# A mixture-of-experts transformer kernel: the routing steps inside attention spread over other engines, and the PSUM banks of scores and maxima exchanged

## The reference

```python
x = x + attention(layernorm(x), Wq, Wkv_down, Wk_up, Wv_up, Wo)       # 8 heads of 32, softmax over 1024 keys
x = x + moe_top2(layernorm(x), gate_w, w1, b1, w2, b2)                # 14 experts, the two best of a softmax
x = x + linear_attention(layernorm(x), Wq, Wk, Wv, Wo)                # 16 heads of 8, cumulative sums
x = x + moe_top1(layernorm(x), router_w, W1, b1, W2, b2)              # 8 experts, capacity 1280
```

```python
probs = softmax(x @ gate_w.T)
top2_p, top2_i = top_k(probs, 2)
w = top2_p / maximum(top2_p.sum(-1, keepdims=True), 1e-10)
moe_out = w[:, 0:1] * out_of(top2_i[:, 0]) + w[:, 1:2] * out_of(top2_i[:, 1])
```

## Time and profile before

| | us |
|---|---|
| median of 3 runs | 2246.83 (2245.2 to 2247.13) |
| profiled execution | 2234.0 |
| its span | 2232.3 |
| mean granted clock of TensorE in it, share of full | 0.887 |
| busy in the span: PE / DVE / ACT / POOL | 1722.2 / 1527.5 / 1177.9 / 1366.9 |

### The profile page before, as it was taken

How to read it: one execution, slowest core, us unless ns; L and a number is a source line. 1 busy time by engine, 2 the same in 40 slices (tenths; PEclk the granted TensorE clock), 3 DMA queues, 4 the chain that set the end, 5 groups by cost and what they waited for, 6 DMA issues and landing times. The chain is left out here.

```text
span 2232.3 us, 54806 instructions
## 1 busy us (share of the span) xinstructions
PE 1722.2 (77%) x18737; PEld 1007.6 (45%) x18737; DVE 1527.5 (68%) x3787; ACT 1177.9 (53%) x2275; POOL 1366.9 (61%) x1088
## 2 busy tenths in 40 slices
PE   7977999998989899898952799377767776100997
PEld 3423455444444444444432688344444443000897
DVE  5756888899889889888835234178888877620453
ACT  4625887877777677777741355224444444021343
POOL 0004777766778777777785233488888872155465
PEclk9977999999999999999975799688999988555999
DMA  4754222221313122222222434400000000132332
GB/s 154 247 170 139 60 69 79 59 81 55 93 57 95 58 72 79 60 90 62 78 78 76 156 125 122 152 21 20 19 19 19 19 19 0 43 114 77 99 102 63
DMA packets 161611, 178.39 MB, mean 80 GB/s; under 512 B 39905, under 2 KB 124776, under 8 KB 161416
## 3 DMA queue, kind: packets, MB, share of 16 engines
q1 hardware_dynamic: 146584, 145.41, 21.3%
q0 software_dynamic: 13824, 29.43, 4.0%
q10 hardware_dynamic: 1008, 0.92, 0.1%
HBM read 97.76 MB, written 78.16 MB: 79 GB/s over the span
## 5 line engine op out<-in xcount | busy, mean ns | idle before, releaser
L941 DVE TENSOR_REDUCE halfmax<-p_m 128x1 f32<-128x512 f32 x1024 | 657.5, 685 | 122.3 <-PE p_m L694 111.0
L922 ACT ACTIVATE probs<-p_s,ESCALE 128x512 f32<-128x512 f32 x1024 | 645.9, 689 | 103.8 <-PE p_s L718 84.5
L632 POOL TENSOR_TENSOR sum_p<-sum_p,probs 128x1024 f32<-128x1024 f32 x192 | 455.7, 2374 | 38.9 <-ACT probs L922 25.4
L694 PE MATMUL p_m<-ka,qa 96*32 96x512 f16 x4096 | 422.6, 396 | 40.2 <-DVE halfmax L941 26.3
L718 PE MATMUL p_s<-qa,ka 98*32 98x512 f16 x4096 | 417.5, 388 | 15.9 <-DMA qa<-max_lo 10.7
L725 PE MATMUL p_o<-probs,vh 128*32 128x256 f32 x4096 | 320.0, 384 | 0.4 <-ACT probs L922 0.4
L632 POOL TENSOR_TENSOR sum_p<-probs 128x1024 f32<-128x1024 f32 x64 | 151.6, 2369 | 217.9 <-ACT probs L922 217.5
L694 PEld LDWEIGHTS p_m<-ka,qa 96*32 96x32 f16 x4096 | 114.3, 95 | 302.8 <-DVE halfmax L941 247.5
L1653 PE MATMUL ln_p_cum<-ln_kv,c_tri 128*128 128x512 f32 (+1 forms) x384 | 169.8, 587 | 89.6 <-POOL ln_kv L1597 89.6
L1306 ACT ACTIVATE e_h<-e_p_h,e_w 128x256 f32<-128x256 f32 x316 | 126.8, 474 | 159.3 <-PE e_p_h L1285 85.3
L718 PEld LDWEIGHTS p_s<-qa,ka 98*32 98x32 f16 x4096 | 118.2, 97 | 112.0 <-ACT probs L922 25.3
(11 more groups left out here) (298 smaller groups left out, 2740.6 us busy)
## 6 DMA issues: line engine op xcount, KB each, us to landing
e_xb<-xs SPq DMA_DIRECT2D x40, 257.0 KB
e_xb<-xs SPq DMA_DIRECT2D x78, 128.0 KB, 2.0
ys<-e_y SPq DMA_DIRECT2D x78, 128.0 KB, 1.9
v<-pj_v SPq DMA_DIRECT2D x8, 1024.0 KB, 5.0
qa<-q SPq DMA_DIRECT2D x64, 128.0 KB
ka<-k SPq DMA_DIRECT2D x64, 128.0 KB
vh<-v SPq DMA_DIRECT2D x64, 128.0 KB
o<-ot SPq DMA_DIRECT2D x64, 128.0 KB
```

The lines of the kernel that those rows point to most:

```text
L632: nc.gpsimd.tensor_tensor(sum_p[i][:, :], (sum_p[i] if n else probs[0])[:, :], probs[k][:, :], ALU.add).then_inc(sum_p_d, 1)
L694: mm = nc.tensor.matmul(max_bank(s, n)[j * DH0:(j + 1) * DH0, :], qa[s][0:KA, (n // 2) * P + j * DH0:(n // 2) * P + (j + 1) * DH0], ka[s][ ...
L922: nc.scalar.activation(probs[k][:, h * HALF:(h + 1) * HALF], score_bank(u % SLOTS, k, h)[:, :], ACT.Exp, scale=ESCALE[:, 0:1]).then_inc(pr ...
L941: nc.vector.reduce_max(halfmax[u % 2][:, n // 2, n % 2:n % 2 + 1], max_bank(u % SLOTS, n)[:, :], AX.X).then_inc(max_read, 1)
```

## The change

The kernel after differs in these points.

- **Banks**: `p_s` has two banks and `p_m` three. `SCORE_BANKS` alternates over two, `MAX_BANKS` rotates over three.
- **`best_two`**: the sums go to `totals`, one column per tile of the whole run; `prob` stays unscaled, and the reciprocal and the scaling fall away there.
- **`find_experts`** keeps the eight `max_index` alone. Two ScalarE copies (`keep_bests`, `keep_chosen`, piece 9) store the two best values in `GATE` and the two indices in `chosen`. **`mark_chosen`** (VectorE, piece 9) writes `hot` by 16 `tensor_scalar` of 14 elements, each comparing `steps`, an iota stored with step 2, with one column of `chosen`. **`join_marks`** (GpSimd, piece 10, behind its fourth sum and its scatter) adds both halves of `hot` into `both`.
- **`count_tiles`** is gone. **`ranks`** moves from piece 11 to 10 and carries the counts in PSUM: one matmul of the identity with `base` (the row numbers reached so far), one of `stri` with `both`, and eight of `ones` with one tile of `both` broadcast over the tiles behind it, 112, 98, ..., 14 columns. The ninth block of `pos_ps` is the new `base`, which ScalarE copies in `keep_base` (piece 12).
- **`find_slots`** moves from piece 12 to 11 and is a product of `hot` with `pos_ps` and one reduction into `tabs["slotf"]`. GpSimd converts these to the integers of `slot`. The scatters start at piece 13 instead of 14.
- **`gates`** runs once, on all tiles, behind `find_rows`. The last matmul for the counts is replaced by `base - start`.
- For the last two batches `mark_experts` does the marks and `both` on VectorE in three instructions.

```diff
-SCORE_BANKS = tuple(i % 3 for i in range(SLOTS * SCORES - 4)) + (0, 1, 0, 2)
-MAX_BANKS = tuple(i % 2 for i in range(SLOTS * RING))
+SCORE_BANKS = tuple(i % 2 for i in range(SLOTS * SCORES))
+MAX_BANKS = tuple(i % 3 for i in range(SLOTS * RING))
...
             def scatter(h, half):
...
+                if n == 0:
+                    pool.wait_ge(places, 2 * b + 2)
+                    nc.gpsimd.tensor_copy(slot[b % NX][:, :], tabs["slotf"][:, b * ST * 2:(b + 1) * ST * 2]).then_inc(slot_d, 1)
                 apart(pool, slot_d, b + 1, passed)
...
+            def join_marks(b):
+                pool.wait_ge(marks_d, b + 1)
+                from_first(pool, pos_d, b)
+                nc.gpsimd.tensor_tensor(both[:, :, :], hot[:, 0, :, :], hot[:, 1, :, :], ALU.add).then_inc(hot_d, 1)
...
                 pe.wait_ge(hot_d, b + 1)
-                pe.wait_ge(seen_d, (b + 1) * ST)
-                nc.tensor.matmul(pos_ps, c["stri"][:, :], both[:, :, :], start=True, stop=False)
-                nc.tensor.matmul(pos_ps, c["ones"][:, :], seen[:, 0:ST, :], start=False, stop=True).then_inc(pos_d, 1)
+                from_first(pe, base_d, b)
+                nc.tensor.matmul(pos_ps, c["ident"][:, :], base[:, :].unsqueeze(1).broadcast_to([P, ST + 1, E0]),
+                                 start=True, stop=False, skip_group_check=True)
+                nc.tensor.matmul(pos_ps[:, 0:ST, :], c["stri"][:, :], both[:, :, :], start=False, stop=False, skip_group_check=True)
+                for t in range(ST):
+                    mm = nc.tensor.matmul(pos_ps[:, t + 1:ST + 1, :], c["ones"][:, :], both[:, t:t + 1, :].broadcast_to([P, ST - t, E0]),
+                                          start=False, stop=(t == ST - 1), skip_group_check=True)
+                mm.then_inc(pos_d, 1)
...
+            def keep_bests(b):
+                act.wait_ge(choice, 2 * b + 2)
+                nc.scalar.copy(GATE[:, b * ST * 2:(b + 1) * ST * 2].rearrange("p (t k) -> p t k", k=2), best[:, :, 0:2]).then_inc(gates_d, 1)
+
+            def keep_chosen(b):
+                act.wait_ge(best_d, b + 1)
+                from_first(act, marks_d, b)
+                nc.scalar.copy(chosen[:, :, :].rearrange("p k t -> p t k"), at[:, :, 0:2]).then_inc(chosen_d, 1)
+
+            def keep_base(b):
+                act.wait_ge(pos_read, b + 1)
+                nc.scalar.copy(base[:, :], pos_ps[:, ST, :]).then_inc(base_d, 1)
...
+            def mark_chosen(b):
+                if b == 0:
+                    dve.wait_ge(set_d, 3)
+                dve.wait_ge(chosen_d, b + 1)
+                from_first(dve, pos_read, b)
+                for k in range(2):
+                    for t in range(ST):
+                        last = nc.vector.tensor_scalar(hot[:, k, t, :], steps[:, :, 0], chosen[:, k, t:t + 1], None, ALU.is_equal)
+                last.then_inc(marks_d, 1)
...
             def find_slots(b):
                 dve.wait_ge(pos_d, b + 1)
-                nc.vector.tensor_tensor(place[:, :, :], pos_ps, start[:, :].unsqueeze(1).broadcast_to([P, ST, E0]), ALU.add).then_inc(pos_read, 1)
+                nc.vector.tensor_tensor(placed[:, :, :, :], hot[:, :, :, :],
+                                        pos_ps[:, 0:ST, :].unsqueeze(1).broadcast_to([P, 2, ST, E0]), ALU.mult).then_inc(pos_read, 1)
                 dve.wait_ge(pos_read, b + 1)
...
+                nc.vector.tensor_reduce(tabs["slotf"][:, b * ST * 2:(b + 1) * ST * 2].rearrange("p (t k) -> p k t", k=2), placed[:, :, :, :],
+                                        AX.X, ALU.add).then_inc(places, 2)
```

More of the change, by code:

```diff
@@ L457, in attend @@
         xT = sb("r_xT", [P, GT])
-        top, total, prob = sb("r_top", [P, G]), sb("r_total", [P, ST]), sb("r_prob", [P, ST, E0])
+        top, totals, sums, prob = sb("r_top", [P, G]), sb("r_totals", [P, TILES]), sb("r_sums", [P, TILES]), sb("r_prob", [P, ST, E0])
+        chosen, steps = sb("r_chosen", [P, 2, ST]), sb("r_steps", [P, E0, 2])
         best, at = sb("r_best", [P, ST, 8]), sb("r_at", [P, ST, 8], U32)
[L460 to L464, removed]
+        hot, both = sb("r_hot", [P, 2, ST, E0]), sb("r_both", [P, ST, E0])
+        now, start, base = sb("r_now", [P, E0]), sb("r_start", [P, E0]), sb("r_base", [P, E0])
+        placed = sb("r_placed", [P, 2, ST, E0])
         zeros = sb("r_zeros", [P, BT // P, D])
@@ L637, in head @@
                         scatter(u, n - 2)
+                    marked = sequence(u, 10)
+                    if n == 3 and marked is not None and marked < B - 2:
+                        join_marks(marked)
             for s in range(SLOTS):
@@ L649, in _ @@
                 normalise(u)
-            for h in range(UNITS, FIRST + 14 + B * H0):
+            for h in range(UNITS, FIRST + 13 + B * H0):
                 for half in range(2):
@@ L904, in behind_tile @@
                         exponentials(b)
+                    b = sequence(h, 9)
+                    if b is not None:
+                        keep_bests(b)
+                        if b < B - 2:
+                            keep_chosen(b)
+                    b = sequence(h, 12)
+                    if b is not None:
+                        keep_base(b)
             act.sem_inc(od_d, OD0)
@@ new lines, in mark_experts @@
+            def mark_experts(b):
+                dve.wait_ge(best_d, b + 1 + (b - B + 2))
+                from_first(dve, pos_read, b)
+                for k in range(2):
+                    last = nc.vector.scalar_tensor_tensor(out=hot[:, k, :, :], in0=at[:, :, k].unsqueeze(2).broadcast_to([P, ST, E0]), scalar=1.0,
+                                                          in1=c["iota"][:, 0:E0].unsqueeze(1).broadcast_to([P, ST, E0]),
+                                                          op0=ALU.mult, op1=ALU.is_equal)
+                last.then_inc(best_d, 1)
+                dve.wait_ge(best_d, b + 2 + (b - B + 2))
+                from_first(dve, pos_d, b)
+                nc.vector.scalar_tensor_tensor(out=both[:, :, :], in0=hot[:, 0, :, :], scalar=1.0, in1=hot[:, 1, :, :],
+                                               op0=ALU.mult, op1=ALU.add).then_inc(hot_d, 1)
@@ L1062, in route @@
                     find_experts(b)
+                b = sequence(gap, 9)
+                if b is not None and b < B - 2:
+                    mark_chosen(b)
                 b = sequence(gap, 1)
@@ L1074, in route @@
                     scales(b)
-                b = sequence(gap, 12)
-                if b is not None:
-                    find_slots(b)
-                b = sequence(gap, 13)
-                if b is not None:
-                    gates(b)
                 b = sequence(gap, 7)
```

123 lines of the change are left out of this document (49 added, 74 removed).

## The result

The changed kernel has a median of 2263.16 us (five runs, 2257.47 to 2264.97), the kernel before 2245.2 beside it. The ratio is 1.0085, 95% interval [1.0055, 1.0115]: slower, where I had forecast 2217 and faster. The profiled execution took 2257.47, against 2234.0 before.

What follows compares the result with a forecast made beforehand. No engine was full, TensorE led at 77%; routing cost 24.3 us a batch. Unit bounds plus 2.5 made 119.75 against 126.3, gaining 33 over 5.1 batches, less 3 for free units: median 2217 us, range 2192 to 2240.

Steps and rivals of the forecast that it cites:

- piece 9 and 1: Units where VectorE makes the marks: its own 11.26, routing 1.87 and marks 2.9, together 16.0 us against 14.95 now.
- the wait of `ranks` for `join_marks`: TensorE waiting for GpSimd's add: costed at nothing, hidden beside the denominators; without that cover up to 1.6 us a batch.
- my bound of 5.6: Upper bound in us for the sixteen marks, one per GpSimd instruction until that queue runs dry; 2.9 was taken.
- rival 1: VectorE's marks go one by one: 2.8 us more in six batches, 17 in all, 2234 us; chance 0.17.
- forecast batch: Eight routed units after the change: 117.25 plus 2.5 for scatters, 119.75 us, 6.5 less than 126.3.
- the free units: 12 units without routing, 12.98 us each against 12.75, losing 0.23 each: 3 us.
- Piece 11: Unit without TensorE routing step, decided by ScalarE's table loads and normalisations: 14.56 plus 0.6, 15.2 us against 21.11.
- The banks: Two score banks delay TensorE's scores behind ScalarE's exponentials by 0.52 us in a free unit: 12.46 becomes 12.98.
- Rival 3: Two score banks tie TensorE to ScalarE in every unit, 0.65 us each, 42 in all: 2259 us, slower; chance 0.09.
- Ranks: TensorE's 10 matmuls, 20 instructions, instead of 4: about 2.6 us at full clock, bounds 1.5 and 4.7.
- The other pieces: Remaining routed units, bound mostly by TensorE, attention or ScalarE: 13.2 to 15.2 us each.
- The 2.5 for scatters: Added 2.5 us per batch because units with scatters ran 0.8 to 1.07 longer than the same piece without.

Runs made afterwards that it cites:

- the run with two marks behind: Changed kernel with two marks of 112 elements for the sixteen, moved behind `add_attention`: 2174.66 us, 0.9886 of the kernel before.
- the run with marks behind: Changed kernel with its sixteen marks moved behind `add_attention` in VectorE's order: 2210.82 us, 1.0051 of the kernel before.
- short sums: Changed kernel, sixteen marks in place, GpSimd's last three sums cut to 8 columns in the six units 9: 2228.35 us, 0.9952 of the kernel before.
- the first set: First four follow-up runs, on one chip with the kernel before beside them, which had a median of 2199.38 us there.
- Old banks: Changed kernel with three score and two maximum banks: 2210.4 us, 1.0047 with sixteen marks; 2203.8 us, 0.981 with two marks behind `add_attention`.
- the second: Next four follow-up runs, on one chip with the kernel before beside them, which had a median of 2246.85 us there.

## Why the prediction was wrong

**The step that failed** is "piece 9 and 1: 11.26 + 1.87 + 2.9 = 16.0 on VectorE". It failed twice.

*As a sum.* I added the marks to VectorE's load, as if only the total mattered. They stand in a queue: `add_attention` and the next maxima behind them, TensorE behind both. I had named the wait of `ranks` for `join_marks` and costed it (rightly) at nothing, but never asked, for `mark_chosen` itself, what is queued behind it. With the marks ahead, TensorE stood 6.13 us, of which 0.41 would be there anyway; against the run with two marks behind, 15.37 + 5.7 = 21.1, and the half clock that follows makes up the remaining 2.8 of 23.89, 1.7 of it in the sixteen matmuls of `attention`. Only the run with marks behind showed that the order is the smaller part.

*As a price.* The marks took 6.43, not 2.9, and past my bound of 5.6. I had the right row, the chain of seven adds at one per GpSimd instruction, and gave it 0.17 as rival 1, because two casts had once got in together. (Of those seven, two waited and the other five ran through in 1.0, as the marks did later.) The bound had the right course, a wait for each GpSimd instruction until its queue runs dry; most of the 0.8 beyond it is that the thirteen that ran undisturbed took 0.13 each, not 0.09. Rival 1 was near on the length (5.7); its 2234 was far too low since it too paid only for length. The Trainium skill ("SBUF — State Buffer", Who interferes with whom) says, of instructions of VectorE and GpSimd that contend for the ports they share, that whoever issues first has them for the whole instruction and the other fully blocks. The traces agree: 6.4 with full sums, 2.23 with short ones. I cited it and yet took the low price.

**What it cost.** The forecast batch was 119.75, the four measured above average 129.2. By the starts of `rowmax`, the 41 routed units of my sum run from 469.26 to 1128.52 in the changed kernel: 659.3 us where 41 units at 119.75 / 8 make 613.7. That is 45.5 more, and the five windows 9 among them, of 23.6 to 24.1 where I had 16.0, hold 39.5 of it. The last batch with marks meets the same stall at the loop's end, behind those units:

```profile
1131.23 6.71 DVE L1052 TENSOR_SCALAR r_hot<-r_steps,r_chosen 128x14 f32<-128x14 f32 x16
...
1138.68 3.66 PE L772 MATMUL p_r<-r_wo,r_oT 128*128 128x128 f32 x16 [6.39 <-DVE X L1001]
```

From 1128.52 to the next stage it takes 134.9; in the kernel before, from the same step (1116.20), 121.1. That is 13.8 more where I had nothing. The 41 units began 3.5 earlier than I had it (469.81 before, and 3 for the free units), so 45.5 + 13.8 - 3.5 = 55.8. The next stage begins 26.1 later than before, where I had it 30 earlier: 56.1, and the account closes. Its first loads, in the changed kernel and in the kernel before:

```profile
1263.41 1.49 SPq L1359 DMA_DIRECT2D e_xb<-xs  x2
```

```profile
1237.32 1.49 SPq L1327 DMA_DIRECT2D e_xb<-xs  x2
```

**What held.**
- *Piece 11*: 15.27 at full clock, forecast 15.2. The largest single gain came as worked out.
- *The banks*: a free unit takes 13.04, forecast 12.98, by the start-up that I had read from the free unit's timeline. Rival 3 (0.48 a unit and more) didn't come.
- *Ranks*: 0.49, then 0.38 and 1.87 with overlaps, 2.4 at full clock; forecast 2.6. At half clock, behind the loop, 0.77 + 0.61 + 3.46. The wait for `join_marks` cost nothing that shows. The changed kernel, in a window of piece 10:

```profile
1028.12 0.49 PE L800 MATMUL p_r<-r_base,c_ident 128*128 128x126 f32 x2
...
1028.44 0.38 PE L802 MATMUL p_r<-r_both,c_stri 128*128 128x112 f32 x2
...
1028.65 1.87 PE L804 MATMUL p_r<-r_both,c_ones 128*128 128x112 f32 x16
```

- *The other pieces*, where the marks don't disturb: pieces 7 to 12 but 9 were forecast at 13.2, 14.85, 15.05, 15.2, 14.1, and the run with two marks behind shows 13.01, 14.97, 15.26, 15.20, 14.23. In the changed kernel itself they are 0.1 to 1.0 over the forecast, and pieces 5 and 6, at 15.47 and 15.58, 1.0 and 1.2.
- *The 2.5 for scatters* isn't a property of the code alone. Outside piece 9 the changed kernel pays 4.7 over my terms without it (105.9 against 101.25). In the first set the same units pay almost nothing: with two marks behind, pieces 5 to 8 take 14.93, 14.14, 13.01 and 14.97, and with 10 to 12 that is 101.7. Old banks show it too: piece 7 takes 12.75 in the first set and 13.77 in the second, though nothing in that unit differs between the two kernels. So units with scatters were longer in the other sets and in both profiles that the forecast was made from and held against, and not in the first, which goes with its shorter times. What differs between the sets stays open.

So with marks as long as I had priced them (2.95), and behind `add_attention`, the plan is worth near what I said: 1.1%, 25 us, where I had 30. One sequence of instructions turned that into a loss of 18 to 22.

## What to carry to other kernels

Before adding small VectorE instructions on SBUF, look at what GpSimd runs at that place: each may cost one whole GpSimd instruction, so their number matters and not their elements; two of 112 elements beat sixteen of 14 by 1.1 to 1.6%. Then price the step by what is queued behind it: list the next instructions on that engine and who waits for each, and compare its length with the lead (here the three maxima banks) that the waiting engine has. And judge banks or buffers again after the work that they covered has moved: these were neutral with the old routing and cost 0.5 to 0.8% with the new.

## What the runs showed of the hardware

- Between GpSimd instructions that ran without a gap (sum 2.4 us, product 0.7, sum) VectorE got in one `tensor_scalar` of 14 elements at a time, or two `scalar_tensor_tensor`, though all sixteen stood ready.
- An indirect scatter on GpSimd (1.01 us) with no sum ready behind it didn't hold VectorE: thirteen marks ran in 1.74 us beside and behind it. With a sum ready behind it, in the run with marks behind, one mark took 3.12 us, through the rest of the scatter and the whole sum. Why the scatter's end counts there, the traces don't show.
- Whether the input has a step of 1 or 2 made no difference (6.37 and 6.43).
- The clock: after TensorE had idled about 6 us, every window shows the half level behind it (16 matmuls of `attention` 3.75 in place of 2.05). After 2 us it went either way in the same kernel (short sums): 1.93 idle and then 2.02 at full clock, 2.05 idle and then 3.65, for 1.9 us more in the window. The length of the wait doesn't decide it, since another of 2.04 kept the full clock and one of 1.94 lost it. What does, these runs don't show.
